# Laying the first cross-attention steps operation by operation between the last gated-slot steps of a fused decoder block, with three batches' scores in other PSUM banks

## The chip, the cores and the metric

The kernel runs on one NeuronCore of one Trainium2 chip, in one launch. The metric is the device time of that launch in microseconds. TensorE (PE; PEld is its weight load), VectorE (DVE), ScalarE (ACT), GpSimd (POOL) and SyncE (SP, which issues the DMAs) each run their own list of instructions in order, and meet only at semaphores. So the order in which a list is written, together with the waits in it, is the schedule.

## The reference

The block takes a stream `x` of 32 sequences, 128 tokens each, 128 wide, in float32:

```
x = x + slot_attention(layernorm(x))                     # 4 heads, 64 slots, a gated recurrence over time
x = x + cross_attention(layernorm(x), ctx, ctx,
        bias = fside + fside, attn_mask, key_padding)    # 16 heads of 8, softmax over 128 keys
x = x + experts(layernorm(x))                            # top 2 of 8, LoRA experts on a shared 512-wide MLP
```

The bias `fside` has its own 128x128 matrix for each batch and each of the 16 heads, so one batch brings 1 MB of it. For the cross attention of one batch that means

```
q = h @ Wq.T + bq;  k = c @ Wk.T + bk;  v = c @ Wv.T + bv          # h = layernorm(x), c = ctx
scores = q.k / sqrt(8) + attn_mask + fside + fside, -inf where padded
out = softmax(scores) @ v;   x = x + out @ Wo.T + bo
```

## The kernel before

`decoder` (L49) has three stages, one after the other: the gated-slot stage (functions `gsa_*`) works on pairs of batches, 16 in all (0 to 15); the cross stage (`x_*`) on single batches, 0 to 31; the expert stage (`f_*`) on groups of four. Each is a software pipeline. In tick `t` of the slot stage the parts belong to different pairs: `gate` works on pair t, `turn` on t-1, `intra` on t-2, `mix` on t-3, `finish` on t-4. In step `n` of the cross stage `norm` works on batch n+3, `project` on n+2, `scores` on n+1, `attend` on n and `finish` on n-1.

The functions for one engine (`gsa_tensor`, `gsa_scalar`, `gsa_vector`, `gsa_pool`, and the same for `x_`) write out one tick or step of that engine. The middle of each stage is a loop (`gsa_loop`, `x_loop`), its ends are written out by `gsa_peeled` and `x_peeled`, which switch off the parts that have no batch. The last slot ticks are 16 (turn, intra, mix, finish), 17 (intra, mix, finish), 18 (mix, finish) and 19 (finish), and the first cross steps are -3 (norm), -2 (norm, project), -1 (and scores) and 0 (and attend). I call this part the passage. In the kernel before it goes, on every engine, by whole steps: tick 16, step -3, tick 17, step -2, tick 18, step -1, tick 19, step 0, step 1, then the loop from step 2.

What the prediction follows, by engine and line:

- DVE: `statistics` and `aggregates` (L1034, L1039) and `normalise` (L1044) give a batch its normed rows, `masks` (L1051) its key mask, `score(i)` (L1026, four instructions of one head each) adds the bias to four heads' scores from one bank, `causal_attention` (L680), `slot_logits`, `slot_maxima` (L687 to L696), `causal_mix` (L714), `slot_sums` and their reciprocal (L702, L708) are the slot stage's.
- POOL: `biases` (L1121) adds mask and bias for a whole batch and writes `c_bias`; `keys_apart` (L1126) lays a batch's keys apart by head; `roots` (L1111, L1114) gives the reciprocal deviation; `slot_products` and `slot_weights` (L794, L802), `squares` (L782), `outputs_normalised` (L788) are the slot stage's. The weights of pair 15 are made in tick 17.
- PE: `all_scores` (L873) writes a batch's scores, one matmul for each of four banks; `inputs_turned` (L880), `queries_keys` (L886), `weights_turned` (L907), `mix_values` (L920), `values` (L892), `outputs` (L896) follow in a step. `attention` (L444), `slot_logits` (L453), `slot_mix` (L476), `outputs` (L486), `project_out` (L499) are the slot stage's.
- ACT: exps of the scores (L954), copies of the turned inputs (L960), keys (L971), queries (L965).
- SP: `x_loads` issues the 1 MB of bias of batch n once the bias tile of batch n-2 has been read (`need(sp, C["fm"], n - 1)`, L1150).

PSUM has eight banks here. The cross stage puts its scores in banks 1, 4, 5 and 6 and its sums in 7, and turns weights through 2 and 3. The slot stage uses 4 and 5 for attention and logits, 6 and 7 for its mix and outputs, 2 and 3 for squares, turned rows and values. Bank 6 is what the last slot pairs and the first scores both want:

```
SCORE_BANKS = (1, 4, 5, 6)                                                       # L860
pe.wait_ge(G["lgts"], PAIRS); pe.wait_ge(G["un"], PAIRS); x_peeled(cross, -1)    # L1694 to L1696
```

## Time and profile before

| | us |
|---|---|
| time, median of 3 runs | 604.25 (603.99 to 606.11) |
| profiled execution, its own time | 605.81 |
| its span, first to last instruction | 604.1 |
| a slot tick in the loop (182.46 to 171.54 on DVE) | 10.9 |
| a cross step in the loop (262.47 to 255.28 on PE) | 7.2 |
| the passage, from PE's first matmul of tick 17 to that of step 2 | 193.57 to 240.58 |

The engines are busy for 542.7 us (PE), 482.7 (DVE), 398.6 (ACT) and 355.7 (POOL) of the span. The profile lists instructions by engine, with the line, the output and input tiles, the start in us from the span's start, the duration, and in brackets how long the engine had stood idle before it and what ended that. The granted clock of TensorE is a share of full speed: 1.00 is 2.4 GHz and 0.50 is 1.2 GHz. Since every list runs in order, an instruction's start is the later of two times: when its engine is free, and when the last thing it waits for is there.

### The profile page before, as it was taken

How to read it: one execution, taken by the hardware profiler on the slowest of the kernel's cores; microseconds unless marked ns; L12 is line 12 of the kernel's file. 1: busy time of each engine (PE TensorE's matmuls, PEld its weight loads, DVE VectorE, ACT ScalarE, POOL GpSimd, SP SyncE). 2: the span in 40 equal slices, each digit the busy share in tenths (PEclk: the TensorE clock that was granted, in tenths of full speed). 3: DMA queues.
4: the chain of work that ended last, by engine and by line, in shares of the span. 5: the costliest groups of instructions: out<-in, count | busy, mean ns of one | idle time of the engine just before them, and what ended most of it. 6: DMA issues, size and time to landing. Idle time of an engine off the chain costs nothing.

```text
span 604.1 us, 17291 instructions
## 1 busy us (share of the span) xinstructions
PE 542.7 (90%) x5328; PEld 416.1 (69%) x5328; DVE 482.7 (80%) x1945; ACT 398.6 (66%) x1033; POOL 355.7 (59%) x362
## 2 busy tenths in 40 slices
PE   4689999999998559999999999999978999999986
PEld 3457777777776436777777777777766778788864
DVE  2478887887886358999999999999988688888872
ACT  2668878878775238889999999999965333333221
POOL 6234555456544657888888888888933233334430
PEclk9799999999998868999999999999987899999999
DMA  6910000000000075898989888888700000000000
GB/s 169 239 21 2 1 1 1 0 0 0 2 0 2 7 126 101 153 168 152 159 155 156 155 155 149 148 151 162 128 3 1 2 17 19 17 17 19 17 19 17
DMA packets 84429, 42.47 MB, mean 70 GB/s; under 512 B 4378, under 2 KB 84132, under 8 KB 84388
## 3 DMA queue, kind: packets, MB, share of 16 engines
q1 hardware_dynamic: 83234, 41.63, 37.5%
q8 instruction: 21, 0.34, 0.3%
q10 hardware_dynamic: 1154, 0.33, 0.2%
q14 instruction: 20, 0.16, 0.1%
HBM read 39.86 MB, written 2.10 MB: 69 GB/s over the span
## 4 chain that ended last, share of the span: by engine, by line
PE 50%; DVE 17%; issue 16%; ACT 7%; POOL 7%; DVEq 0%; ACTq 0%; POOLq 0%
PE banks L873 6%; PE banks L907 6%; PE banks L920 5%; PE banks L453 5%; ACT c_P L954 4%; PE banks L1228 4%; DVE c_P L1026 3%; DVE shared L714 3%; PE banks L1252 3%; PE banks L896 3%; PE banks L417 2%; PE banks L444 2%; PE banks L499 2%; PE banks L886 2%; DVE banks L687 2%
## 5 line engine op out<-in xcount | busy, mean ns | idle before, releaser
L1121 POOL TENSOR_TENSOR c_bias<-c_fside,c_cm 128x2048 f32<-128x2048 f32 x32 | 146.2, 4568 | 27.5 <-PE banks L873 16.9
L954 ACT ACTIVATE c_P<-c_P,c_min 128x128 f32<-128x128 f32 x512 | 156.7, 391 | 2.9 <-DVE c_min L1026 2.9
L1026 DVE CUSTOM_DVE_ANT_0 c_P<-banks,c_bias 128x128 f32<-128x128 f32 x512 | 116.4, 284 | 5.6 <-issue 3.0
L907 PEld LDWEIGHTS banks<-ident,c_P 128*128 128x128 f32 x512 | 59.3, 144 | 30.0 <-issue 23.2
L907 PE MATMUL banks<-ident,c_P 128*128 128x128 f32 x512 | 76.0, 282 | 3.7 <-DVE shared L1062 3.7
L1062 DVE COPY shared<-banks 128x512 f32<-128x512 f32 x96 | 65.7, 685 | 0.0
L1228 PE MATMUL banks<-um,lb_s 128*128 128x512 f32 x192 | 56.1, 407 | 2.7 <-ACT shared L1285 1.9
L1464 POOL TENSOR_TENSOR xs<-shared,xs 128x512 fp32r<-128x512 f32 x8 | 10.7, 1337 | 69.9 <-ACT xs L1295 69.9
L1285 ACT ACTIVATE shared<-banks,bi_col 128x512 f32<-128x512 f32 x32 | 22.0, 687 | 39.2 <-PE banks L1228 39.2
L1228 PEld LDWEIGHTS banks<-um,lb_s 128*128 128x128 f32 x192 | 34.6, 190 | 19.1 <-ACT shared L1285 12.5
L794 POOL TENSOR_TENSOR shared<-shared 128x512 f32<-128x512 f32 x16 | 20.4, 1275 | 38.1 <-ACT shared L585 38.1
L1026 DVE DVE_READ_ACCUMULATOR2_ANT c_min<- 128x1 f32 x512 | 42.6, 83 | 0.0
L873 PE MATMUL banks<-shared,c_q 32*128 32x512 f32 x256 | 38.3, 668 | 1.2 <-DVE X L727 0.5
L453 PEld LDWEIGHTS banks<-shared 128*128 128x128 f32 x256 | 29.8, 191 | 12.8 <-DVE shared L680 12.8
L920 PE MATMUL banks<-shared,c_vpad 128*32 128x128 f32 x1024 | 34.9, 277 | 0.0
L1126 POOL TENSOR_TENSOR shared<-c_k,k_mask 128x512 f32<-128x512 f32 x32 | 33.3, 1042 | 1.8 <-ACT c_k L971 1.8
L920 PE MATMUL banks<-shared,c_ones 128*32 128x128 f32 x1024 | 33.8, 273 | 0.0
L453 PE MATMUL banks<-shared 128*128 128x64 f32 x256 | 31.9, 278 | 1.7 <-DVE shared L680 1.7
L1290 ACT COPY shared<-banks 128x512 f32<-128x512 f32 x8 | 4.7, 587 | 43.6 <-PE banks L1202 43.6
L1252 PE MATMUL banks<-woT,shared 128*128 128x128 f32 x256 | 30.7, 278 | 2.1 <-DVE shared L1414 1.9
L1414 DVE SCALAR_TENSOR_TENSOR shared<-banks,neg_bi,shared 128x512 f32<-128x512 f32 x32 | 23.5, 749 | 11.0 <-PE banks L1228 10.7
L1252 PEld LDWEIGHTS banks<-woT,shared 128*128 128x128 f32 x256 | 29.2, 192 | 4.1 <-DVE shared L1414 4.1
(195 smaller groups left out, 1310.6 us busy)
## 6 DMA issues: line engine op xcount, KB each, us to landing
c_fside<-in_fside_Bx16xSxS_dram SPq DMA_DIRECT2D x64, 512.0 KB, 7.2
c_ctx<-in_ctx_dram SPq DMA_DIRECT2D x32, 64.0 KB, 5.2
out_dram<-shared SPq DMA_DIRECT2D x8, 256.0 KB, 2.3
X<-in_x_dram SPq DMA_DIRECT2D x3, 512.0 KB, 5.4
kmask_sb<-in_mask_BxS_bf_dram SPq DMA_DIRECT2D x1, 512.0 KB, 6.8
X<-in_x_dram SPq DMA_DIRECT2D x2, 128.0 KB, 3.0
c_P<-in_L_ffn_wi_dram SPq DMA_DIRECT2D x1, 256.0 KB
c_P<-in_L_ffn_lora_B_dram SPq DMA_DIRECT2D x1, 256.0 KB
```

The source lines that it names most:

```text
L453: last = nc.tensor.matmul(bank(4)[:, 256 * b + GM * h:256 * b + GM * h + GM], Am[:, 4 * (h // 2) + 2 * b + h % 2, :], sp_[:, q, b, GM * h: ...
L873: nc.tensor.matmul(bank(SCORE_BANKS[i]), qx[rows, o, :], kbd[rows, o, :, :].rearrange("p j s -> p (j s)"), start=True, stop=True).then_inc ...
L907: last = nc.tensor.transpose(bank(2 + i % 2)[:, 128 * j:128 * j + 128], P[:, q, XG * i + j, :], ident[:])
L920: last = nc.tensor.matmul(bank(7)[32 * i:32 * i + 32, 128 * w:128 * w + 128], block, PTs[:, o, i, 128 * j:128 * j + 128], start=(j == 0), ...
L954: last = nc.scalar.activation(P[:, par, h, :], P[:, par, h, :], ACT.Exp, bias=mn[:, par, h:h + 1], scale=-1.0)
L1026: last = nc.vector.tensor_tensor_reduce(out=P[:, o, h, :], in0=bank(SCORE_BANKS[i])[:, 128 * j:128 * j + 128], in1=fm[:, o, h, :], scale=- ...
L1062: nc.vector.tensor_copy(PTs[:, q, i, :], bank(2 + i % 2)).then_inc(C["ptD"], 1)
L1121: nc.gpsimd.tensor_tensor(fm[:, q, :, :], fs[:, q, :, :], bc(cm[:], XH), ALU.add).then_inc(C["fm"], 1)
L1126: nc.gpsimd.tensor_tensor(kbd[:, q, :, :], bc(kx[:], XG), inner(k_mask[:], 128), ALU.mult).then_inc(C["kbd"], 1)
L1228: last = nc.tensor.matmul(out, weight[:, a, :], moving[:, b, :], start=start and k == 0, stop=stop and k == len(PASSES) - 1, **also)
L1252: last = nc.tensor.matmul(bank(7)[:, 128 * b:128 * b + 128], hT[:, c, 128 * b:128 * b + 128], woT[:, c, :], start=(c == 0), stop=(c == FC ...
L1414: nc.vector.scalar_tensor_tensor(hT[:, c, :], bank(2 + c % 2), neg_bi[:, c:c + 1], r1[:, c, :], ALU.max, ALU.add).then_inc(M["h"], 1)
```

## The change

Each engine function takes a new argument `only`, a tuple of names, and lets a part run only if its name is in it, so that one tick or step can be laid down in several pieces. With that the passage is written out anew on all four engines:

- On POOL the bias and the keys of batch 0 come ahead of tick 17, and the bias and keys of batch 1 ahead of pair 15's slot weights, which come after them. Step -3's roots go ahead of tick 16.
- On DVE statistics, norm and mask of batches 0 and 1 stand between parts of ticks 16 and 17, and the scores of batch 0 follow straight on the slot sums of pair 15. Tick 18 is spread through steps 0 and 1, tick 19 follows step 2.
- On PE the inputs and queries of batch 0 stand before the logits of pair 15, the scores of batch 0 between slot mix and slot outputs of pair 14, and ticks 18 and 19 are spread through steps 0 to 2 with the waits that the shared banks need.
- ACT follows PE.
- The scores of batches 0, 1 and 2 go to banks 1, 4, 5, 1, so bank 6 stays with the slot stage. The fourth matmul therefore waits until DVE has read the first one's result.
- `masks` moves from the start of a step (for batch n+2) to the end of the step before (batch n+3), where the norm of the same batch is.
- Two more cross steps are written out ahead of the loop and two fewer behind it: the loop has as many rounds.

```diff
+def named(only):
+    return lambda flag, name: flag and (only is None or name in only)
...
+        FIRST_BANKS = (1, 4, 5, 1)
+        FIRST = 3
+        def score_banks(batch):
+            return FIRST_BANKS if isinstance(batch, int) and batch < FIRST else SCORE_BANKS
...
+                places = score_banks(n + 1)
                 for i in range(NI):
                     rows = slice(32 * i, 32 * i + 32)
-                    nc.tensor.matmul(bank(SCORE_BANKS[i]), qx[rows, o, :], kbd[rows, o, :, :].rearrange("p j s -> p (j s)"),
+                    if places[i] in places[:i]:
+                        need(pe, C["tt"], 4 * n + 5 + places.index(places[i]))
+                    nc.tensor.matmul(bank(places[i]), qx[rows, o, :], kbd[rows, o, :, :].rearrange("p j s -> p (j s)"),
                                      start=True, stop=True).then_inc(C["sc"], 1)
...
             def masks():
-                need(dve, C["fm"], n + 2)
-                km = kmask_sb[:, bass.ds((n + 2) * T, T)]
+                need(dve, C["fm"], n + 3)
+                km = kmask_sb[:, bass.ds((n + 3) * T, T)]
...
-            with engine.Fori(1, B // 2 - 3, 2) as m:
+            with engine.Fori(2, B // 2 - 3, 2) as m:
... POOL
             pool.wait_ge(G["xn"], PAIRS)
             x_peeled(cross, -3)
-            gsa_peeled(gsa, PAIRS + 1)
+            gsa_peeled(gsa, PAIRS)
...
             x_peeled(cross, -2)
+            gsa_peeled(gsa, PAIRS + 1, "outputs")
+            x_peeled(cross, -1)
+            gsa_peeled(gsa, PAIRS + 1, "squares")
+            gsa_peeled(gsa, PAIRS + 1, "weights")
+            x_peeled(cross, 0)
             gsa_peeled(gsa, PAIRS + 2)
-            x_peeled(cross, -1)
+            x_peeled(cross, 1)
             gsa_peeled(gsa, PAIRS + 3)
... ACT
-            x_peeled(cross, -3)
-            gsa_peeled(gsa, PAIRS + 1)
+            gsa_peeled(gsa, PAIRS + 1, "turned", "roots")
             x_peeled(cross, -2)
-            gsa_peeled(gsa, PAIRS + 2)
+            gsa_peeled(gsa, PAIRS + 1, "exps", "outputs")
             x_peeled(cross, -1)
+            x_peeled(cross, 0, "exps1", "exps2", "inputs", "exps3")
+            gsa_peeled(gsa, PAIRS + 2, "turned")
+            x_peeled(cross, 0, "exps0", "keys", "queries", "turned3")
+            gsa_peeled(gsa, PAIRS + 2, "roots")
+            x_peeled(cross, 1, "exps1")
+            gsa_peeled(gsa, PAIRS + 2, "outputs")
+            x_peeled(cross, 1, "exps2", "inputs", "exps3", "exps0", "sums", "keys", "queries", "turned3")
             gsa_peeled(gsa, PAIRS + 3)
... DVE
-            x_peeled(cross, -3)
-            gsa_peeled(gsa, PAIRS + 1)
+            x_peeled(cross, -3, "statistics", "aggregates")
+            gsa_peeled(gsa, PAIRS)
             dve.wait_ge(s_km, 16)
-            x_peeled(cross, -2)
-            gsa_peeled(gsa, PAIRS + 2)
-            x_peeled(cross, -1)
+            x_peeled(cross, -3, "normalise", "masks")
+            gsa_peeled(gsa, PAIRS + 1, "attention")
+            x_peeled(cross, -2, "statistics", "aggregates")
+            gsa_peeled(gsa, PAIRS + 1, "logits")
+            x_peeled(cross, -2, "normalise", "masks")
+            gsa_peeled(gsa, PAIRS + 1, "mix", "sums")
+            x_peeled(cross, -1, "scores0", "scores1", "scores2", "scores3")
+            gsa_peeled(gsa, PAIRS + 1, "stream")
+            x_peeled(cross, -1, "statistics", "aggregates", "values", "normalise", "masks")
+            x_peeled(cross, 0)
+            gsa_peeled(gsa, PAIRS + 2, "mix")
+            x_peeled(cross, 1, "statistics", "scores0")
+            gsa_peeled(gsa, PAIRS + 2, "stream")
...
... PE
-            x_peeled(cross, -3)
-            gsa_peeled(gsa, PAIRS + 1)
+            gsa_peeled(gsa, PAIRS + 1, "attention", "turned", "squares")
             pe.wait_ge(G["silu"], PAIRS)
             x_peeled(cross, -2)
-            gsa_peeled(gsa, PAIRS + 2)
-            pe.wait_ge(G["lgts"], PAIRS)
+            gsa_peeled(gsa, PAIRS + 1, "logits", "mix")
+            pe.wait_ge(G["shift"], PAIRS)
+            x_peeled(cross, -1, "scores")
+            gsa_peeled(gsa, PAIRS + 1, "outputs", "project")
+            x_peeled(cross, -1, "inputs", "queries", "values")
+            x_peeled(cross, 0, "scores")
+            pe.wait_ge(G["rt"], PAIRS - 2)
+            x_peeled(cross, 0, "turned0", "inputs")
+            pe.wait_ge(G["x1"], PAIRS - 2)
+            x_peeled(cross, 0, "turned1", "queries")
+            gsa_peeled(gsa, PAIRS + 2, "turned")
+            x_peeled(cross, 0, "turned2", "turned3", "values")
+            pe.wait_ge(C["ptD"], 3)
+            gsa_peeled(gsa, PAIRS + 2, "squares", "mix")
+            x_peeled(cross, 1, "scores")
+            pe.wait_ge(C["ptA"], 1)
+            gsa_peeled(gsa, PAIRS + 2, "outputs", "project")
...
+            pe.wait_ge(C["ptD"], 6)
+            gsa_peeled(gsa, PAIRS + 3, "squares")
             pe.wait_ge(G["un"], PAIRS)
+            x_peeled(cross, 2, "scores")
...
```

In the changed file the lines stand lower: L1121 is L1141, L1126 is L1146, L873 is L894, L794 and L802 are L805 and L813, L486 and L499 are L491 and L504.

The list of POOL in the passage before, from the weights of pair 15 (L794, L802) to the bias of batch 1; `shared<-shared` are tiles of the slot stage:

```order
L794 TENSOR_TENSOR shared<-shared 128x512 [waits g_ppTp,g_p]
L802 TENSOR_TENSOR shared<-shared 128x512 [waits g_ri,g_pe]
L782 TENSOR_TENSOR shared<-shared 128x256 [waits g_ss,g_un]
L1121 TENSOR_TENSOR c_bias<-c_fside,c_cm 128x2048 [waits c_cm,vector_constants_made,c_fside_loaded0,transposed_weights_copied,cross_weights_loaded]
L1126 TENSOR_TENSOR shared<-c_k,k_mask 128x512 [waits c_k]
L1111 TENSOR_TENSOR vareps<-meanvar,eps_tile 128x1 [waits c_rstd,c_aggr]
L1114 TENSOR_TENSOR rstd<-vareps,minus_half 128x1 [waits c_xn,c_vareps]
L788 TENSOR_TENSOR shared<-shared 128x256 [waits g_y,g_r]
L782 TENSOR_TENSOR shared<-shared 128x256 [waits g_ss,g_un]
L1121 TENSOR_TENSOR c_bias<-c_fside,c_cm 128x2048 [waits c_fside_loaded1,c_cm]
```

And in the changed kernel, from the bias of batch 0 to the weights of pair 15, behind which the bias of batch 2 follows:

```order
L1141 TENSOR_TENSOR c_bias<-c_fside,c_cm 128x2048 [waits c_cm,vector_constants_made,c_fside_loaded0,transposed_weights_copied,cross_weights_loaded]
L1146 TENSOR_TENSOR shared<-c_k,k_mask 128x512 [waits c_k]
L1131 TENSOR_TENSOR vareps<-meanvar,eps_tile 128x1 [waits c_rstd,c_aggr]
L1134 TENSOR_TENSOR rstd<-vareps,minus_half 128x1 [waits c_xn,c_vareps]
L799 TENSOR_TENSOR shared<-shared 128x256 [waits g_y,g_r]
L1141 TENSOR_TENSOR c_bias<-c_fside,c_cm 128x2048 [waits c_fside_loaded1,c_cm]
L1146 TENSOR_TENSOR shared<-c_k,k_mask 128x512 [waits c_k]
L1131 TENSOR_TENSOR vareps<-meanvar,eps_tile 128x1 [waits c_rstd,c_aggr]
L1134 TENSOR_TENSOR rstd<-vareps,minus_half 128x1 [waits c_xn,c_vareps]
L793 TENSOR_TENSOR shared<-shared 128x256 [waits g_ss,g_un]
L805 TENSOR_TENSOR shared<-shared 128x512 [waits g_ppTp,g_p]
L813 TENSOR_TENSOR shared<-shared 128x512 [waits g_ri,g_pe]
```

The bias of batch 0 (the first `c_bias` row) now stands ahead of all of tick 17, and pair 15's products and weights (L805, L813) have gone behind the bias and keys of batch 1.

The list of PE before, from the slot mix of pair 14 (L476) to the first scores (L873):

```order
L476 MATMUL banks<-shared 128x128 [waits g_un,g_sT,g_ppT]
L476 MATMUL banks<-shared 128x128 x7
L486 MATMUL banks<-shared 32x128 [waits g_v,g_bm]
L486 MATMUL banks<-shared 32x128 x7
L499 MATMUL banks<-g_wo_sb,shared 128x128 [waits g_v,g_onT]
L499 MATMUL banks<-g_wo_sb,shared 128x128
L873 MATMUL banks<-shared,c_q 128x512 [waits c_q,c_kbd,g_un,g_lgts]
L873 MATMUL banks<-shared,c_q 128x512 x3
```

And in the changed kernel, from the logits of pair 15 to the scores of batch 1:

```order
L458 MATMUL banks<-shared 128x64 [waits g_am]
L458 MATMUL banks<-shared 128x64 x7
L481 MATMUL banks<-shared 128x128 [waits g_un,g_sT,g_ppT]
L481 MATMUL banks<-shared 128x128 x7
L894 MATMUL banks<-shared,c_q 128x512 [waits c_kbd,c_q,g_shift]
L894 MATMUL banks<-shared,c_q 128x512 x2
L894 MATMUL banks<-shared,c_q 128x512 [waits c_tt]
L491 MATMUL banks<-shared 32x128 [waits g_v,g_bm]
L491 MATMUL banks<-shared 32x128 x7
L504 MATMUL banks<-g_wo_sb,shared 128x128 [waits g_v,g_onT]
L504 MATMUL banks<-g_wo_sb,shared 128x128
L901 MATMUL banks<-ident,c_xn 128x128 [waits c_ctx_loaded1,c_xn]
```

The first scores (L894) have moved up from behind tick 18 to behind the slot mix of pair 14. They are now three matmuls and a fourth behind a wait of its own on `c_tt`, which DVE raises when it has read the first bank.

## Rows read from the trace of the kernel before

**Rows 1.** The page: granted clock in 40 slices of the span, and the bias loads

```profile
PEclk9799999999998868999999999999987899999999
...
c_fside<-in_fside_Bx16xSxS_dram SPq DMA_DIRECT2D x64, 512.0 KB, 7.2
```

**Rows 2.** Busy time by stretch: length, busy time of each engine, clock, DMA share

```profile
193.57:240.58 47.01, 32.41 (x269) 23.16 (x269) 26.98 (x136) 21.64 (x67) 31.58 (x27) 0.78 0.41 74
240.58:283.50 42.92, 40.89 (x596) 30.93 (x596) 40.12 (x252) 38.92 (x131) 36.96 (x23) 1.00 0.91 158
213.32:217.40 4.08, 4.08 (x29) 2.06 (x29) 0.83 (x3) 0.37 (x1) 1.72 (x2) 0.52 1.03 153
225.63:231.60 5.97, 5.97 (x30) 4.43 (x30) 4.20 (x27) 2.37 (x9) 4.52 (x1) 0.56 0.51 85
```

**Rows 3.** PE's timeline: start, duration, engine, line, operation, idle time before

```profile
193.57 1.14 PE L444 MATMUL banks<-shared 64*128 64x256 f32 x8
...
197.16 2.00 PE L453 MATMUL banks<-shared 128*128 128x64 f32 x16 [1.44 <-DVE shared L680]
...
202.53 0.64 PE L486 MATMUL banks<-shared 128*32 128x128 f32 x16 [2.28 <-DVE shared L714]
...
203.75 0.42 PE L880 MATMUL banks<-ident,c_xn 128*128 128x128 f32 x1
...
213.32 1.08 PE L486 MATMUL banks<-shared 128*32 128x128 f32 x16 [4.57 <-DVE shared L714]
...
215.49 1.97 PE L873 MATMUL banks<-shared,c_q 32*128 32x512 f32 x8
217.38 0.33 PE L880 MATMUL banks<-ident,c_xn 128*128 128x128 f32 x1
...
225.63 2.09 PE L873 MATMUL banks<-shared,c_q 32*128 32x512 f32 x8 [0.52 <-DVE X L727]
...
233.42 1.14 PE L873 MATMUL banks<-shared,c_q 32*128 32x512 f32 x8 [0.36 <-issue]
...
240.58 1.14 PE L873 MATMUL banks<-shared,c_q 32*128 32x512 f32 x8
```

**Rows 4.** DVE's timeline, norm of batch 0 to first scores

```profile
194.01 0.28 DVE L1034 BATCH_NORM_STATS2 stats<-X 128x6 f32<-128x128 f32 x1
194.45 0.18 DVE L1039 BATCH_NORM_AGGREGATE meanvar<-stats 128x2 f32<-128x6 f32 x1 [0.15 <-DVE stats L1034]
...
203.11 0.20 DVE L708 RECIPROCAL shared<-shared 128x8 f32<-128x8 f32 x1
...
211.40 0.74 DVE L1044 TENSOR_SCALAR c_xn<-X,meanvar,rstd 128x128 f32<-128x128 f32 x1 [6.23 <-POOL rstd L1114]
212.06 1.21 DVE L714 TENSOR_TENSOR shared<-banks,mask_b 128x1024 f32<-128x1024 f32 x1
...
217.64 0.29 DVE L1026 CUSTOM_DVE_ANT_0 c_P<-banks,c_bias 128x128 f32<-128x128 f32 x1 [1.22 <-issue]
...
217.86 0.28 DVE L1026 CUSTOM_DVE_ANT_0 c_P<-banks,c_bias 128x128 f32<-128x128 f32 x1
```

**Rows 5.** ACT's timeline, keys of batch 1

```profile
219.79 0.35 ACT L971 ACTIVATE c_k<-banks,bk_col 128x128 f32<-128x128 f32 x1
```

**Rows 6.** POOL's timeline, slot weights of pair 15 to the bias of batch 2

```profile
202.09 1.27 POOL L794 TENSOR_TENSOR shared<-shared 128x512 f32<-128x512 f32 x1 [4.42 <-ACT shared L585]
...
205.08 4.51 POOL L1121 TENSOR_TENSOR c_bias<-c_fside,c_cm 128x2048 f32<-128x2048 f32 x1
209.56 1.03 POOL L1126 TENSOR_TENSOR shared<-c_k,k_mask 128x512 f32<-128x512 f32 x1
210.55 0.18 POOL L1111 TENSOR_TENSOR vareps<-meanvar,eps_tile 128x1 f32<-128x1 f32 x1
...
211.33 0.72 POOL L788 TENSOR_TENSOR shared<-shared 128x256 f32<-128x256 f32 x1
...
225.98 4.52 POOL L1121 TENSOR_TENSOR c_bias<-c_fside,c_cm 128x2048 f32<-128x2048 f32 x1 [2.14 <-DVE c_cm L1051]
```

More of the change, by code:

```diff
@@ L534, in gsa_normalise, with gsa_scalar @@
             last.then_inc(G["xn"], 1)
-        def gsa_scalar(act, t, par, gate, turn, intra, mix, finish, ahead):
+        def gsa_scalar(act, t, par, gate, turn, intra, mix, finish, ahead, only=None):
             def x_turned():
@@ L805, in roots_ahead, with gsa_peeled @@
                 gsa_rstd(pool, t + 1)
-            if ahead:
+            on = named(only)
+            if on(ahead, "roots"):
                 roots_ahead()
-            if finish:
+            if on(finish, "outputs"):
                 outputs_normalised()
-            if intra:
+            if on(intra, "weights"):
                 slot_products()
-            if turn:
+            if on(turn, "heads"):
                 heads_apart()
-            if intra:
+            if on(intra, "weights"):
                 slot_weights()
-            if mix:
+            if on(mix, "squares"):
                 squares()
-        def gsa_peeled(tick, t):
-            tick(t, t % 2, *(0 <= t - k < PAIRS for k in (0, 1, 2, 3, 4, -1)))
+        def gsa_peeled(tick, t, *only):
+            tick(t, t % 2, *(0 <= t - k < PAIRS for k in (0, 1, 2, 3, 4, -1)), only or None)
         def gsa_loop(engine, tick):
@@ L1698, in _ @@
+            gsa_peeled(gsa, PAIRS + 3, "squares")
+            pe.wait_ge(G["un"], PAIRS)
+            x_peeled(cross, 2, "scores")
+            pe.wait_ge(G["rt"], PAIRS)
+            x_peeled(cross, 2, "turned0", "inputs", "turned1", "mix", "queries", "turned2", "turned3", "values", "outputs")
+            pe.wait_ge(C["ptA"], 3)
+            gsa_peeled(gsa, PAIRS + 3, "project")
+            x_peeled(cross, 3, "scores", "turned0", "inputs")
             pe.wait_ge(G["x1"], PAIRS)
-            for n in range(0, 2):
-                x_peeled(cross, n)
+            x_peeled(cross, 3, "turned1", "mix", "queries", "turned2", "turned3", "values", "outputs")
@@ L1701, in _ @@
             x_loop(pe, cross)
-            for n in range(B - 6, B - 2):
+            for n in range(B - 4, B - 2):
                 x_peeled(cross, n)
```

283 lines of the change are left out of this document (146 added, 137 removed).

## The prediction

> **What bounds the kernel now.** I read the strips of the page first. The granted clock is at full level in nearly all of the span and drops in the slices that hold the passage, near slices 13 to 16 of 40 [rows 1]. The busy times by stretch say why. In the 47.01 us of the passage, from PE's first matmul of slot tick 17 to its first of cross step 2, PE is busy 32.41, DVE 26.98, ACT 21.64 and POOL 31.58. In the 42.92 us after it PE is busy 40.89 and DVE 40.12 [rows 2]. So the steady cross stage is full, and no engine is full in the passage: it is a chain that hops between engines. The timelines of the engines give the chain. PE finishes the mix of pair 15, and its slot outputs start only at 213.32, after 4.57 us without work, "released by DVE" [rows 3]. DVE's instruction ahead of that was itself held: the norm of batch 1 waited 6.23 us, until 211.40, for a reciprocal deviation from POOL [rows 4]. POOL made that at 210.55, behind 4.51 us of bias and 1.03 of keys for batch 0, and it began that bias only at 205.08, behind the slot weights of pair 15 [rows 6]. PE idle then lowers its clock: in the 4.08 us after the idle time it is granted 0.52, the lower level of 1.2 GHz, though PE is wholly busy there. The 5.97 us from 225.63 are at 0.56 [rows 2]. Slot outputs take 0.64 us at 202.53 and 1.08 at 213.32, four scores 1.14 at 240.58 and 1.97 and 2.09 earlier [rows 3].
>
> **The change part by part.** Nothing is computed that was not before. The instructions are the same but for waits. So I follow the chain through the new order and compare three milestones with the old ones: first scores on DVE (217.64), start of the bias of batch 2 (225.98), and PE's first matmul of step 2 (240.58).
>
> First leg, to the scores of batch 0. Statistics of batch 0 ahead of tick 16's attention cost that tick 0.28 + 0.15 + 0.18 = 0.6 us on DVE [rows 4]; I take 0.5 of it as late, so tick 17 starts at 194.1 instead of 193.57 [rows 3]. PE now has attention, weights, squares and then inputs and queries of batch 0 ahead of the logits of pair 15. I estimate 3.2 us of work for these (attention is 1.14 of it [rows 3]) and 0.9 of wait for ACT, which copies the inputs behind two slot parts. The logits start at about 198.2 instead of 197.16. From their start to the end of the slot sums' reciprocal the old order took 203.31 - 197.16 = 6.15 [rows 3, 4]. The new one puts norm and mask of batch 1 between, some 0.6. The reciprocal is done at 198.2 + 6.15 + 0.6 = 205.0. The scores of batch 0 follow at once, since their bias, started near 195.1 when DVE has made norm and mask, took 4.51 and was done at 199.7, and the keys at 200.7 [rows 6]. First scores: 205.0 instead of 217.64, 12.6 us earlier. Bounds: 0.5 us less late if the wait for ACT is nothing, 1 us more if the two waits add up.
>
> Second leg, to the bias of batch 2. PE has sent three matmuls and stands at the fourth, which wants bank 1 again, until DVE has read it: four heads that start 0.22 us apart (217.86 - 217.64 [rows 4]), to 205.85. Behind that matmul on PE stand the slot outputs and projection of pair 14, and then the inputs of batch 1, so this wait is on the chain. It costs 0.85 us plus the matmul of 0.3 to 0.5. Outputs and projection took 203.75 - 202.53 = 1.22 mostly at the upper clock and 215.49 - 213.32 = 2.17 at the lower one. From the inputs' turn to batch 1's keys on ACT went 220.14 - 217.38 = 2.76 [rows 3, 5], and keys apart are 1.03 on POOL [rows 6]. Together 205.85 + 0.4 + (1.22 to 2.17) + 2.76 + 1.03 = 211.3 to 212.2. POOL then makes the roots (211.33 - 210.55 = 0.78), and squares, products and weights of pair 15, which before lay one behind the other from 202.09 to 205.08, 2.99. The bias of batch 2 starts at 215.1 to 216.0 instead of 225.98: 10 to 10.9 earlier [rows 6]. What hid behind POOL before is not lost: pair 15's weights are now ready some 10 us later than before, at 215, and PE wants them in step 0 only behind the queries of batch 2, about 216 to 218.
>
> Third leg, to step 2. PE starts the scores of batch 1 at 211.4 to 212.3. Step 0 took 233.42 - 225.63 = 7.79 on PE, mostly at the lower clock [rows 3]. It gets a wait for the fourth score (0.85) and the turn of pair 15's weights, which I put like the slot outputs at 0.64 or 1.08: 9.3 to 9.7. So 220.7 to 222.0. Squares and mix of pair 15 add an estimated 1.3 to 2 (twice the slot outputs at the upper level, not quite that at the lower), to 222.0 to 224.0. Then comes the longest wait of the new order: PE puts three scores of batch 2 and needs DVE to do causal mix (1.21), statistics (0.28) and four heads (0.85) [rows 4] before the fourth. That ends at 224.4 to 226.4. The fourth, outputs and projection of pair 15 are 1.5 to 2.7 (225.9 to 229.1). The rest of step 1 is a whole step less its scores. A steady step is 7.15, from 42.92 us for six [rows 2, 3], so 6.0, and 2 more if its first half is at the lower clock. With squares of 0.5 the scores of batch 3 start at 232.4 to 237.6, against 240.58. I take the middle, 235.0, since of the waits on PE in the old order about half were followed by the lower clock and the new ones are shorter. Gain: 5.6 us. Bounds: 8.2 and 3.0.
>
> After it. Projection of pair 15 (0.6) and its addition on DVE (0.4) now lie in steps 2 and 3, where PE and DVE are nearly full, so I give back 0.7. The early masks are the same instruction in the same place of a steady step (end of one step, start of the next), so nothing there. The remaining stages are as before. The net is 5.6 - 0.7 = 4.9 us.
>
> The profiled execution took 605.81, and the median of the runs is 604.25. The sum is made within the first, 605.81 - 4.9 = 600.9, and I apply the same difference to the median: **599.4 us**.
>
> Loads are no limit. The bias of batch 2 is now issued at about 199.8 instead of 209.75, takes 7.2 [rows 1], and is wanted at 215. That of batch 4 is issued near 220 and wanted near 234. POOL's bias does not slow beside a busy DVE: 4.51 us with DVE idle at 205.08, 4.52 at 225.98 with DVE busy 4.20 of 5.97 us [rows 2, 6].
>
> **The rivals.**
>
> A. The clock stays at the upper level throughout. For it: the new waits on PE are at most 2.5 us, where the old ones before the low stretches were up to 4.57 [rows 3]. Against it: there are about six of them. The sum then ends at its lower bound, 8.2 less 0.7 to 0.0, 596 to 597.
>
> B. The clock stays at the lower level through the passage, and the kernel is slower. PE's list now alternates short pieces with waits for DVE and ACT, instead of resting once and then working densely. From 229.1, where the upper bound has PE after pair 15's projection, the remaining 6.0 us of step 1 take 12.0, and squares 1: 242.1, 1.5 later than before. With half of step 2 also at the lower clock 3.5 more and 0.7 of projection are added: 5.7 slower, 610. I put this case at 608. It decides from the point where low clock lasts past 229 into two dense steps. In the old trace 5.97 us of dense work from 225.63 at 0.56 were followed by full clock [rows 2], which speaks against it.
> By the Trainium skill (TensorE: Matmul & The Clock Gate, "A second HAM failure mode: psum-queue depth-cycling"), a PE that idles briefly and often between groups of matmuls is throttled and released again and again, and pays in throughput. By that rule the sum would lie between my upper bound and this rival, at 602 to 608; its chance is within the one I give B. The trace has so far only the other kind, one long rest and then low clock.
>
> C. What is won is taken back by the tail of pair 15. Its outputs' copy on ACT stands ahead of two groups of exps of step 1, its squares on POOL ahead of the bias of batch 3, and its roots ahead of step 2. If each holds its engine by 1.5 us more than I have, step 2 starts at 239, and the time is 603 to 604: no change. Half of the old passage's loss was of this kind (4.57 and 6.23 us [rows 3, 4]).
>
> D. The order is not what it says, because a wait on a shared bank (`g_shift`, `g_x1`) keeps the first scores where they were. Against it: `g_shift` of pair 15 is raised at about 202.4, before PE needs it. It would be 604.
>
> **How the numbers follow.** Forecast 0.56, A 0.17, B 0.09, C 0.14, D 0.04. About 0.5% (3 us) is what a measurement can tell from no change. Faster than 601.2 are A and the forecast: 0.73. Within 0.5% are D and nearly all of C: 0.17. Slower are B and the bad end of C: 0.10. The forecast's own range is 596.7 to 601.9. To hold 8 in 10 it goes a little further to both sides, from 596.0 (A) to 603.0 (part of C), and leaves out B.
>
> **What would show it.** In the profile after, DVE's first score starts near 205, POOL's bias of batch 0 near 195 and of batch 2 near 215 to 216, and PE's scores of batch 3 near 235. The length of the passage falls from 47.0 to about 41, PE's busy time in it stays about 30, and steps from 4 on are 7.15 apart as before. PE shows waits of about 2.5 us in front of the fourth score of batches 0 and 2, ended by DVE. The forecast is wrong if the bias of batch 2 starts after 219, if the clock reads 0.5 over more than half of the passage, or if steps in the loop are not 7.15.

## The result and the profile after: 676.1 us, 11.6% slower

| | before | after |
|---|---|---|
| time, median of 4 runs each, us | 605.18 (603.99 to 608.08) | 676.10 (673.88 to 676.22) |
| ratio, 95% interval | | 1.1155 [1.1107, 1.1204] |
| span of the profiled execution, us | 604.1 | 674.2 |
| mean granted clock over it | | 0.911 |

The forecast was 599.4 us, and no case of it held such a time. The passage did become shorter, by a little. About 72 us were lost behind it, in the loop of the cross stage, whose work the change leaves as it was.

The page of the kernel after, busy share and granted clock in 40 slices of the span, the queues of instruction packets (packets, MB, share of the DMA engines' time), and three groups of section 5 (busy time, mean ns, idle time ahead of them and what ended it):

```profile
DVE  2678888888765689749378385593898778888872
...
PEclk9799999999995799969869689597899789999999
...
q14 instruction: 45, 0.37, 0.2%
q8 instruction: 21, 0.34, 0.2%
...
L928 PE MATMUL banks<-ident,c_P 128*128 128x128 f32 x512 | 86.6, 307 | 59.1 <-DVE shared L1083 58.8
...
L1047 DVE DVE_READ_ACCUMULATOR2_ANT c_min<- 128x1 f32 x512 | 42.5, 83 | 25.6 <-issue 25.6
...
L1055 DVE BATCH_NORM_STATS2 stats<-X 128x6 f32 (+1 forms) x32 | 9.3, 292 | 36.2 <-issue 36.1
```

Before, the clock was at full level for the whole cross loop (the nines in slices 17 to 29 [rows 1]). Now DVE's strip falls again and again behind slice 16, and the clock falls with it. PE waits 58.8 us for DVE's copies, and DVE itself waits 36.1 and 25.6 us in two groups for nothing that the profile shows ("issue"). There are 45 instruction packets on queue 14, where the kernel before had 20; queue 8 has 21 in both.

DVE's waits in the cross loop, by the instruction that had to wait (us in total, times, longest):

```profile
DVE stats L1055 <- issue: 36.1, 5, 7.4
DVE c_min L1047 <- issue: 25.6, 5, 6.1
```

Five each, and the loop has six rounds of four steps, so five jumps back. (In the kernel before, DVE waited 1.1 us in all at its five jumps.) One of the five places of now, on DVE's timeline (start, duration, engine, line, operation, idle time before):

```profile
283.10 0.28 DVE L1072 SCALAR_TENSOR_TENSOR c_cm<-kmask_sb,half_mask 128x128 f32<-128x128 f32 x1
290.55 0.30 DVE L1055 BATCH_NORM_STATS2 stats<-X 128x6 f32 x1 [7.17 <-issue]
291.00 0.29 DVE L1047 CUSTOM_DVE_ANT_0 c_P<-banks,c_bias 128x128 f32<-128x128 f32 x1 [0.16 <-issue]
...
295.42 0.08 DVE L1047 DVE_READ_ACCUMULATOR2_ANT c_min<- 128x1 f32 x1 [3.92 <-issue]
```

The mask is the last instruction of a round and the statistics are the first of the next. Between them DVE does nothing for 7.17 us, then it runs four instructions (statistics, two heads and one read), and then nothing for 3.92. The second wait is in the middle of a pair, between a head and the read of its accumulator, where the program has no wait. Of the packets on queue 14, one falls in 287 to 288 us and one in 293 to 294, so one lies within each of the two waits. PE's timeline at the same place, and the two waits and a longer stretch by busy time (length; PE, PEld, DVE, ACT, POOL; granted clock, DMA share, GB/s):

```profile
286.54 0.71 PE L907 MATMUL banks<-c_xcT,x_wT 128*128 128x128 f32 x4
296.66 1.11 PE L928 MATMUL banks<-ident,c_P 128*128 128x128 f32 x4 [9.40 <-DVE shared L1083]
```

```profile
283.38:290.55 7.17, 3.88 (x82) 3.28 (x78) 0.00 (x0) 2.01 (x7) 4.54 (x1) 1.00 0.93 158
291.50:295.42 3.92, 0.00 (x0) 0.00 (x0) 0.01 (x1) 0.00 (x0) 0.00 (x0) 0.50 1.16 176
...
253.24:510.00 256.76, 193.83 (x2589) 145.34 (x2589) 174.99 (x1077) 170.26 (x566) 161.05 (x102) 0.85 0.63 109
```

And the stretch of the kernel before that matches the longer one:

```profile
255.28:440.00 184.72, 177.92 (x2588) 134.75 (x2588) 173.38 (x1077) 169.81 (x566) 160.88 (x102) 1.00 0.87 151
```

In the second wait no engine computes. Only the DMA engines are full. Over the loop PE is granted 0.85, where it had 1.00.

From the scores of batch 5 to those of batch 31 PE took 442.17 - 255.28 = 186.89 us before and 512.10 - 253.24 = 258.86 now, 71.97 more. DVE's two waits are 61.7 of it. The other 10.3 are not measured apart. The lower clock can account for them: the 2589 matmuls in this stretch (2588 recorded before) had 177.92 us of busy time before and have 193.83 now. Up to batch 5 the new order and an earlier start had won 2.04, and 71.97 - 2.04 = 69.93 is nearly all of the 70.1 by which the spans differ.

**The passage after.** POOL, DVE and PE:

```profile
194.21 4.52 POOL L1141 TENSOR_TENSOR c_bias<-c_fside,c_cm 128x2048 f32<-128x2048 f32 x1 [0.54 <-DVE c_cm L1072]
...
210.33 1.04 POOL L1146 TENSOR_TENSOR shared<-c_k,k_mask 128x512 f32<-128x512 f32 x1 [4.24 <-ACT c_k L992]
...
215.03 4.52 POOL L1141 TENSOR_TENSOR c_bias<-c_fside,c_cm 128x2048 f32<-128x2048 f32 x1
```

```profile
203.46 0.29 DVE L1047 CUSTOM_DVE_ANT_0 c_P<-banks,c_bias 128x128 f32<-128x128 f32 x1
```

```profile
192.56 1.13 PE L449 MATMUL banks<-shared 64*128 64x256 f32 x8
...
204.45 1.12 PE L894 MATMUL banks<-shared,c_q 32*128 32x512 f32 x2 [2.45 <-DVE c_min L1047]
...
211.47 2.08 PE L894 MATMUL banks<-shared,c_q 32*128 32x512 f32 x6
215.19 2.07 PE L894 MATMUL banks<-shared,c_q 32*128 32x512 f32 x2 [1.63 <-DVE c_min L1047]
...
224.03 0.60 PE L498 MATMUL banks<-shared,same_head 128*128 128x256 f32 x2
...
228.08 1.12 PE L894 MATMUL banks<-shared,c_q 32*128 32x512 f32 x2 [1.29 <-DVE c_min L1047]
...
237.94 1.14 PE L894 MATMUL banks<-shared,c_q 32*128 32x512 f32 x8
```

```profile
205.00:210.00 5.00, 4.39 (x28) 2.77 (x26) 2.74 (x23) 2.03 (x7) 1.09 (x1) 0.55 0.26 45
210.00:215.00 5.00, 2.85 (x8) 1.04 (x8) 3.10 (x11) 2.84 (x10) 4.51 (x6) 0.50 1.02 186
215.00:220.00 5.00, 4.82 (x15) 3.31 (x16) 1.79 (x12) 1.23 (x5) 4.55 (x2) 0.50 0.18 28
...
192.75:237.94 45.19, 35.06 (x265) 24.52 (x264) 28.04 (x134) 19.95 (x61) 30.78 (x24) 0.77 0.43 78
```

First scores and the bias of batch 2 come 14.2 and 10.95 us earlier than before [rows 4, 6], but the scores of batch 3 only 2.6 earlier (237.94 against 240.58 [rows 3]). The slot stage of this execution was itself 0.8 earlier at DVE's mask product of pair 13 (171.89 against 172.68), ahead of anything that the change moves. So the gain of the passage is 1.85 us in this execution, and its length, from PE's first matmul of tick 17 to that of step 2, is 45.4 us where about 41 was forecast. PE is at 0.50 to 0.55 for the 15 us from 205 to 220, it is at 0.72 once more in 230 to 235, and it meets a wait for the fourth score in each of the three batches.

### The profile page after: what moved, and what is told of

The parts are those of the page before. It is cut to its first block, busy times and chain, and to the rows that moved or that the text cites. A ratio compares the mean times of both kernels' runs of the same rounds, so it can differ in the third digit from the quotient of the medians.

```text
span 674.2 us, 17292 instructions
## 1 busy us (share of the span) xinstructions
PE 561.0 (83%) x5328; PEld 427.9 (63%) x5328; DVE 485.8 (72%) x1945; ACT 398.7 (59%) x1033; POOL 356.8 (53%) x362
## 4 chain that ended last, share of the span: by engine, by line
PE 54%; DVE 16%; issue 16%; ACT 10%; POOL 1%; DVEq 1%; ACTq 0%; POOLq 0%
PE banks L1250 10%; PE banks L928 6%; ACT c_P L975 5%; PE banks L941 5%; PE banks L1274 5%; PE banks L458 4%; PE banks L894 4%; DVE c_P L1047 3%; DVE shared L723 2%; PE banks L917 2%; PE banks L422 2%; PE banks L449 2%; PE banks L907 2%; DVE banks L696 1%; DVE shared L702 1%
## 5 line engine op out<-in xcount | busy, mean ns | idle before, releaser
L1141 POOL TENSOR_TENSOR c_bias<-c_fside,c_cm 128x2048 f32<-128x2048 f32 x32 | 146.0, 4563 | 33.7 <-PE banks L894 17.7
L928 PE MATMUL banks<-ident,c_P 128*128 128x128 f32 x512 | 86.6, 307 | 59.1 <-DVE shared L1083 58.8
L928 PEld LDWEIGHTS banks<-ident,c_P 128*128 128x128 f32 x512 | 65.9, 157 | 91.5 <-DVE shared L1083 58.1
L1146 POOL TENSOR_TENSOR shared<-c_k,k_mask 128x512 f32<-128x512 f32 x32 | 33.4, 1045 | 69.3 <-ACT c_k L992 69.1
L1047 DVE DVE_READ_ACCUMULATOR2_ANT c_min<- 128x1 f32 x512 | 42.5, 83 | 25.6 <-issue 25.6
L894 PE MATMUL banks<-shared,c_q 32*128 32x512 f32 x256 | 46.5, 733 | 6.6 <-DVE c_min L1047 5.4
L805 POOL TENSOR_TENSOR shared<-shared 128x512 f32<-128x512 f32 x16 | 20.4, 1277 | 34.2 <-ACT shared L591 34.2
L1055 DVE BATCH_NORM_STATS2 stats<-X 128x6 f32 (+1 forms) x32 | 9.3, 292 | 36.2 <-issue 36.1
```

The source lines that it names most:

```text
L894: nc.tensor.matmul(bank(places[i]), qx[rows, o, :], kbd[rows, o, :, :].rearrange("p j s -> p (j s)"), start=True, stop=True).then_inc(C["s ...
L928: last = nc.tensor.transpose(bank(2 + i % 2)[:, 128 * j:128 * j + 128], P[:, q, XG * i + j, :], ident[:])
L1047: last = nc.vector.tensor_tensor_reduce(out=P[:, o, h, :], in0=bank(score_banks(n + 1)[i])[:, 128 * j:128 * j + 128], in1=fm[:, o, h, :], ...
L1141: nc.gpsimd.tensor_tensor(fm[:, q, :, :], fs[:, q, :, :], bc(cm[:], XH), ALU.add).then_inc(C["fm"], 1)
L1146: nc.gpsimd.tensor_tensor(kbd[:, q, :, :], bc(kx[:], XG), inner(k_mask[:], 128), ALU.mult).then_inc(C["kbd"], 1)
```

## The experiments

Two theories were tried for the loop. F (fetch): on a jump back DVE's instructions must be loaded again, because its loop has another place in its list of instructions. An increment of a semaphore put at the head of the list is one instruction that does no work, so it only moves what stands behind it. L (layout): the new order itself, or the mask at the end of a step, makes DVE wait. In the compiled program the cross loop of DVE has 283 instructions of 64 bytes in both kernels. It begins at instruction 470 before and at 587 after. Each ratio below is to executions of the kernel before that were taken together with that run.

**e1: the order of before, only DVE's loop one round later (it begins at 586)**

```diff
-            for n in range(0, 2):
+            for n in range(0, 4):
                 x_peeled(cross, n)
-            x_loop(dve, cross)
-            for n in range(B - 6, B - 2):
+            x_loop(dve, cross, 2)          # first round; 1 before
+            for n in range(B - 4, B - 2):
```

> The kernel before, with one edit on VectorE's list alone: cross steps 2 and 3 written out ahead of the loop and two fewer behind it, so that the loop's body (283 compiled instructions) begins at instruction 586 instead of 470. Passage, banks and all other engines are as before. Theory F (fetch: after the change the body lies so over the blocks in which VectorE's instructions are loaded that each jump back finds its target gone) expects the loss of the changed kernel here too: five stalls of about 12 us on VectorE at the jump back, about 25 more loads on the instruction queue q14, and 660 to 680 us. Rival L (the new order of the passage or the banks disturb the steady cross stage) expects 604 us, no stalls, 20 loads.

Measured: 659.48 us (659.19 to 659.78), ratio 1.0888 [1.0863, 1.0913], with 45 packets on queue 14 and five waits at the jumps:

```profile
DVE c_cm L1051 <- issue: 35.7, 5, 7.3
```

Without a single instruction of the new passage, the loss is there. Here the waiting instruction is the mask, which in this order is the first of a step. So the wait goes with the jump, and not with the instruction that stands behind it.

**e2: the changed kernel with 43 semaphore increments at the head of DVE's list**

```diff
+            for _ in range(43):
+                dve.sem_inc(s_passed, 1)
             dve.wait_ge(s_x[0], 16)
```

> The changed kernel with 43 semaphore increments put ahead of VectorE's first wait, which only move its list by 43 instructions: the loop begins at 630 instead of 587, so at the same place within a block of 128 as in the kernel before (470 = 86 modulo 128, 630 = 118 modulo 128; 502 + 128 would be the same as before plus a block, so the place is 32 later than in before). F expects the stalls gone if this place is good: 600 to 604 us. If the blocks are of 256 and only the place modulo 256 counts, it may be still bad: 660 to 680. L expects 676 us in any case.

Measured: 606.68 us (604.71 to 609.29), ratio 1.0022 [1.0006, 1.0038], 20 packets on queue 14, granted clock 1.00 from 250 to 440. In 280 to 320 us this kernel has one such packet, and the changed kernel has five; in 320 to 400 this one has none:

```profile
q14 instruction: 1, 0.01, 0.1%
...
q14 instruction: 5, 0.04, 0.5%
```

Nothing of the new order was altered, and 69 us came back. F is shown and L has fallen. It also shows what the change is worth without the fetches: nothing, or a loss of 0.2%. (The expectation calls the place "the same within a block of 128"; by its own numbers, 86 and 118, it is not. The forecasts of F and L do not hang on that.)

**e8: the kernel before with 117 increments at the same place, so that its loop begins at 587**

```diff
+            for _ in range(117):
+                dve.sem_inc(s_passed, 1)
```

> The kernel before with 117 semaphore increments at the head of VectorE's list and nothing else, so that its cross loop begins at instruction 587 of the list, where the changed kernel has it. Fetch theory: the loop is fetched again at each of 6 jumps back, and the time is 655 to 680 us, with two waits per round of about 7 and 5 us on VectorE ended by nothing that the profile shows, and about 45 instruction packets instead of 20. Rival (the new order of the work itself makes the waits, or the jump of a longer prologue does): 604 to 608 us, since the order is that of before.

Measured: 664.62 us (662.93 to 666.31), ratio 1.0993 [1.0954, 1.1032], 46 packets. (Six rounds have five jumps back, not the six of the expectation.) The kernel before is slowed by place alone. Its waits, and the two of the first jump by stretch:

```profile
DVE c_cm L1051 <- issue: 34.8, 5, 7.7
...
DVE c_min L1026 <- issue: 6.6, 5, 1.6
```

```profile
279.31:284.64 5.33, 3.99 (x82) 3.28 (x78) 0.00 (x1) 2.24 (x8) 0.00 (x0) 1.00 1.11 192
285.61:287.20 1.59, 0.00 (x0) 0.00 (x0) 0.00 (x1) 0.00 (x0) 1.59 (x1) 1.00 0.00 0
```

The first wait costs about as much as in the changed kernel (7.0 us on average against 7.2), the second 1.3 instead of 5.1. In the stretch shown the DMA engines are idle in the second wait, where in the changed kernel they were full of bias loads (DMA share 0.00 against 1.16). That a fetch is slow because it comes behind the loads fits this pair, but the first wait here had the DMA engines full too (1.11) and is the shortest of the five (5.33), and no run altered the loads alone. So the cause of the longer second wait is open.

**e3 and e4: the changed kernel and the one before with DVE's loop of 2 steps per round, 12 rounds**

```diff
-            x_loop(dve, cross)
+            x_loop(dve, cross, 1)      # two steps a round on DVE alone
```

> The changed kernel, with VectorE's loop of two cross steps a round instead of four (12 rounds; body 143 compiled instructions instead of 283); the other engines' loops as they are. F expects no stall, since so short a body stays loaded wherever it lies: 600 to 604 us, the instruction loads back to about 20. What the passage alone brings then shows: the trace of the changed kernel has step 4 only 1.25 us ahead of the kernel before, when both are set on tick 14, so 603. L expects 676 us.

> The control to that: the kernel before with the same short loop on VectorE. F and L both expect 604 to 606 us: twice the jumps, at about 0.3 us each and mostly hidden.

Measured: e3 607.65 us (605.94 to 609.71), ratio 1.003 [1.0015, 1.0045]; e4 608.03 (606.86 to 610.07), ratio 1.004 [1.0026, 1.0054]. A loop of 143 instructions is not fetched again at place 587 (20 packets) and costs 0.4% in e4, where it only adds six jumps. It cures the changed kernel as the increments do, and the two differ by 0.4 us, with intervals that overlap: the new passage alone is worth next to nothing.

**e5: 11 increments instead of 43, the loop begins at 598**

```diff
+            for _ in range(11):
+                dve.sem_inc(s_passed, 1)
```

> The changed kernel with 11 semaphore increments (43 in the earlier one) at the head of VectorE's list. Its cross loop then begins at instruction 598 of the list instead of 587. Fetch theory with blocks of 8 KB (128 instructions), as the packets have it: the loop lies at place 86 of a block like in the kernel before, spans as few blocks as there, and nothing is fetched at a jump back: 605 to 608 us, no waits of 7.2 and 5.1 us. Fetch theory with blocks of 16 KB (256 instructions): place 86 of 256 against 214 in the kernel before, so the loop's 283 instructions span two blocks here as well and the result is also 605 to 608; but if one block of a pair is kept ahead, it stays at 670 to 676. Rival: not the place of the loop but something that 43 extra instructions did by their time at the start: 11 of them do a quarter of it, so 640 to 676.

Measured: 605.52 us (605.50 and 605.54), ratio 1.0016 [0.9985, 1.0046], 20 packets. Eleven places do all that 43 did, so it is a border and not the time that the increments take. For the loop of 283, places 586 (e1) and 587 are bad; 470, 598 and 630 are good. The run did not separate blocks of 8 KB from blocks of 16 KB, since both fit all five places.

That settled the 70 us. The other question was why the passage gained 1.85 us and not 5.6. Theory W: the waits for the fourth score are on the chain. Theory C: the low clock ate it. To compare kernels, I measure from DVE's mask product of pair 13.

**e6: own banks for the first scores, on top of e2**

```diff
-        FIRST_BANKS = (1, 4, 5, 1)
+        FIRST_BANKS = ((1, 4, 5, 2), (1, 4, 5, 6), (1, 4, 5, 1))
...
+            pe.wait_ge(G["rt"], PAIRS - 2)          # before the scores of batch 0
+            pe.wait_ge(G["un"], PAIRS - 1)          # before those of batch 1
+            pe.wait_ge(C["tt"], 8)                  # before the squares of pair 15
```

> The changed kernel with 43 increments at the head of VectorE's list (so without its loss in the loop, 606.7 us) and other banks for the first scores: 1, 4, 5, 2 for batch 0, 1, 4, 5, 6 for batch 1, 1, 4, 5, 1 for batch 2, with the waits on earlier readers of banks 2 and 6 that this needs. The waits of 2.45 and 1.63 us ahead of the fourth scores of batches 0 and 1 go. Theory W (these waits are on the chain that sets the end of the passage): keys of batch 1 and with them the bias of batch 2 on GpSimd start 2 to 2.5 us earlier than 215.0, scores of batch 3 at 235.5 to 236.5 instead of 238.5, time 603.5 to 605. Theory C (the low clock and the later waits on ScalarE and GpSimd set it): bias of batch 2 at most 1 us earlier, scores of batch 3 at 237.5 to 239, time 606 to 607.5.

**e7: dummy transposes where PE waits, on top of e2**

```diff
+        WARM = {-1: 10, 0: 7, 1: 6}
+        def warm(count):
+            for _ in range(count):
+                nc.tensor.transpose(bank(2)[:, 0:128], ident[:], ident[:])
...
+                        warm(WARM[n])           # before the wait for the fourth score
...
+            warm(5)                             # before the scores of batch 0
...
+            warm(4)                             # before its values
```

> The changed kernel with 43 increments at the head of VectorE's list (606.7 us) and dummy transposes into bank 2 on TensorE where it waits in the passage: 10, 7 and 6 ahead of the fourth scores of batches 0, 1 and 2, 5 ahead of the scores of batch 0 and 4 ahead of its values. Their results are never read. Theory C (the low clock of 205 to 225 us ate the gain): granted clock over 0.9 in 205 to 225, scores of batch 3 at 234 to 236 instead of 238.5, time 603 to 604.5. Theory W (the chain goes by waits for other engines, and the clock matters little): clock high, but scores of batch 3 at 238 to 239 and time 606 to 608. If the dummy work delays the work behind it and the clock stays at 0.5: 607 to 610.

**e10: of e6 only batch 0's own bank; e9: e6 with 11 dummy transposes into bank 7**

```diff
-        FIRST_BANKS = ((1, 4, 5, 2), (1, 4, 5, 6), (1, 4, 5, 1))
+        FIRST_BANKS = ((1, 4, 5, 2), (1, 4, 5, 1), (1, 4, 5, 1))      # e10
...
-            x_peeled(cross, -1, "inputs", "queries", "values")
+            x_peeled(cross, -1, "inputs")                             # e9, banks as in e6
+            warm(3)
+            x_peeled(cross, -1, "queries")
+            warm(6)
+            x_peeled(cross, -1, "values")
+            warm(2)
```

> The kernel with own banks for the first scores (600.5 us, ratio 0.994), but batch 1 again in banks 1, 4, 5, 1; only batch 0 has its own fourth bank. It tells which of the two waits was worth the 6 us. If it is batch 0's wait (behind it stand slot outputs of pair 14 and the inputs and keys of batch 1, for which GpSimd waits): ratio 0.994 to 0.997, the bias of batch 2 on GpSimd 4 to 4.6 us earlier against tick 16 of the slot stage than with the shared bank. If both matter alike: 0.998. If it is batch 1's: 1.001 or more.

> The kernel with own banks for the first scores (600.5 us, ratio 0.994) and 11 dummy transposes into bank 7 on TensorE, 3 after the inputs of batch 1, 6 after its queries, 2 after its values, where it waits for ScalarE; their results are never read. The clock there was granted 0.52 in 210 to 215 and 0.80 in 215 to 220. If short idle time still lowers the clock there and this is on the chain: clock near 1.0 in 210 to 220, scores of batch 2 to batch 3 unchanged but both 1 to 1.5 us earlier against tick 16, ratio to before 0.991 to 0.993. If the chain goes over GpSimd there (busy 28.2 of 35 us): no change, 0.993 to 0.996, or worse if the dummy work delays the scores of batch 1.

Measured, times in us; the two milestones are counted from the mask product of pair 13 and come from one execution of each kernel:

| kernel | time | ratio to before | bias of batch 2 | scores of batch 3 |
|---|---|---|---|---|
| before | | | 53.3 | 67.9 |
| changed kernel | 676.10 | 1.1155 [1.1107, 1.1204] | 43.1 | 66.05 |
| e2 | 606.68 | 1.0022 [1.0006, 1.0038] | 45.1 | 66.0 |
| e7 dummy work | 603.81 | 0.9981 [0.9960, 1.0002] | 43.4 | 64.3 |
| e10 bank of batch 0 | 601.15 | 0.9929 [0.9902, 0.9956] | 40.8 | 62.4 |
| e6 banks of 0 and 1 | 600.50 | 0.9944 [0.9920, 0.9969] | 40.5 | 58.6 |
| e9 e6 and dummy work | 600.29 | 0.9903 [0.9879, 0.9926] | 40.5 | 60.6 |

Two rows of e6, POOL's keys of batch 1, and PE's scores of batch 1:

```profile
209.74 1.04 POOL L1145 TENSOR_TENSOR shared<-c_k,k_mask 128x512 f32<-128x512 f32 x1
```

```profile
211.04 2.09 PE L893 MATMUL banks<-shared,c_q 32*128 32x512 f32 x8 [0.32 <-POOL shared L1145]
```

POOL's wait of 4.24 us for the keys is gone, because PE goes straight on to the slot outputs and the inputs of batch 1. The clock of e6, e7 and e9 by stretch, in this order:

```profile
205.00:210.00 5.00, 3.09 (x34) 1.64 (x30) 4.96 (x31) 2.85 (x10) 4.79 (x2) 1.00 1.07 174
210.00:215.00 5.00, 4.62 (x19) 2.88 (x20) 4.11 (x18) 2.62 (x10) 4.12 (x6) 0.52 0.78 148
215.00:220.00 5.00, 3.53 (x22) 3.19 (x21) 4.71 (x32) 3.92 (x13) 5.00 (x3) 0.80 0.52 75
```

```profile
205.00:210.00 5.00, 3.89 (x32) 2.52 (x31) 4.47 (x35) 0.37 (x1) 3.69 (x1) 0.84 0.84 126
210.00:215.00 5.00, 4.49 (x19) 2.81 (x17) 1.58 (x5) 4.32 (x15) 2.25 (x4) 0.50 0.50 109
215.00:220.00 5.00, 5.00 (x16) 2.33 (x12) 2.47 (x11) 0.17 (x1) 4.92 (x4) 0.50 0.76 114
```

```profile
210.00:215.00 5.00, 3.94 (x26) 2.31 (x26) 4.11 (x20) 3.68 (x13) 4.12 (x6) 1.00 0.77 148
215.00:220.00 5.00, 2.73 (x16) 1.85 (x16) 4.79 (x31) 2.76 (x8) 5.00 (x3) 1.00 0.51 74
220.00:225.00 5.00, 4.11 (x24) 2.28 (x22) 3.00 (x9) 2.06 (x6) 2.03 (x4) 0.66 0.79 154
```

How far can one execution's milestones be trusted? The bias of batch 2 differs by 2 us between e2 and the changed kernel, whose passages are the same, while their scores of batch 3 agree within 0.1. But e3 has this passage too, and its step 2 comes at 240.82 - 172.28 = 68.5, which is 2.5 later than in them. Its clock was low there:

```profile
230.00:235.00 5.00, 5.00 (x32) 3.55 (x30) 1.55 (x7) 2.24 (x8) 2.65 (x2) 0.51 0.01 3
```

So a difference under about 2.5 us in the last column says nothing, and where the milestones and the ratios disagree, the ratios of many runs decide.

W holds and was worth more than I had expected: 7.4 us at step 2 for two waits of 2.23 and 1.63, and 0.8% by the ratios (1.0022 against 0.9944). Batch 0's bank alone brings nearly all of the earlier bias of batch 2. At step 2 it brings 3.6 us of the 7.4, but its ratio is no worse than that of e6, so a gain in time from batch 1's own bank is not shown. Of C, e7 did not get the clock up beyond 210 us, so it tested only the 5 us before that. Its 1.7 us at step 2 are within what one execution can be off; its ratio is below that of e2, with intervals that just miss each other (1.0002 and 1.0006). In e9 the dummy work did keep the clock at 1.00 until 220, but it fell to 0.66 right after, and step 2 came 2.0 later than in e6. The intervals of e6 and e9 overlap (0.9920 to 0.9926), so which of them is faster is open. Both, and e10, beat the kernel before. How much of the 7.4 us is the waits themselves and how much the clock that they bring down is not separated either. In e6 there is one stretch of 5 us at 0.52 and one at 0.80, where e2 has three at the lower level (0.52, 0.50 and 0.50 from 205 to 220).

## Why the prediction was wrong

**The step that failed** is the sentence "The remaining stages are as before". I had followed the order of instructions on each engine through the passage and had taken the loop as a constant, steps 7.15 apart. The change text itself says that two more steps are written out ahead of the loop. I read that as a matter of which steps are where, and not as a shift of the loop by 117 instructions in DVE's list. In the runs this shift costs 52 us up to the scores of batch 31 with the old order (e8: 502.7 - 263.9 = 238.8 from batch 5 to 31, against 186.9) and 72 with the new one. All rivals were about the passage too, so none could reach 676. Of the signs that I had named against the forecast, "if steps in the loop are not 7.15" is the one that came true: the four steps of a round in the changed kernel take 18.9, 8.3, 7.3 and 7.2 us (scores at 282.35, 301.21, 309.48, 316.81 and 324.00).

What could have warned was on the page of before, with its 20 packets on queue 14, and in the times of those: none between 269 and 412 us, so from the first jump back on the loop ran without a fetch. A loop that runs without one is a property that a longer head can take away.
The Trainium skill has the rule ("Runtime: NRT & Kernel Launch", section "Instruction fetch mechanics"): most engines hold two blocks of 16 KiB, 256 instructions each, fetched ahead in sequence only, and a taken branch out of them stalls for a fetch. Worked out from that page's figures, as an estimate: 283 instructions lie in two blocks unless the loop begins in the last 26 places of one (2 x 256 - 283 = 229). The five places measured agree with this if a border lies 76 to 86 instructions behind a multiple of 256 in the compiled list. No run measured where the borders are. The packets here are 8 KB (0.37 MB in 45), half of that page's block. The page gives no price for such a stall.
In the changed kernel the price was 61.7 us of waits in five jumps, 12.3 each.

**Leg 1 was right.** First scores at 203.46, forecast 205.0; taken from the mask product of pair 13 the miss is 0.75.

**Leg 2 was right** in this execution; in e2, with the same passage, the bias of batch 2 came 1.9 later (45.1 against 43.1 in the table), which is past my bounds. The bias of batch 2 at 215.03, forecast 215.1 to 216.0, the wait for the fourth score 2.45 us, forecast about 2.5. The scores of batch 1 started at 211.47, forecast 211.4 to 212.3.

**Leg 3 had the right pieces and a wrong size.** Step 0 up to the squares of pair 15 took 224.03 - 211.47 = 12.6 us, where I had put 9.3 to 9.7. I had taken the old step 0 of 7.79 us [rows 3] and added one wait and one turn. It had a wait of 1.63 for its fourth score, and the clock was at 0.50 until 220. What came behind, from the squares to step 2, took 13.9, against 11.7 to 15.6 forecast. So step 2 came at 237.94 instead of 235.0, 0.3 outside my bounds. The gain was 1.85 instead of 5.6, and by steps 3 and 4 it is down to 1.2, so the give-back of 0.7 was about right. The term that was mis-sized in the passage is step 0, by about 3 us. Over the whole kernel the runs without fetches put it between 1.3 us lost (e2, ratio 1.0022) and 0.4 won (e3 against e4), that is nothing.

**The rivals.** The passage itself landed on C's figure ("step 2 starts at 239, and the time is 603 to 604: no change"), but not by C's mechanism. Pair 15's tail did hold GpSimd, whose squares stood 4.16 us for ScalarE's copy until 230.56, with the bias of batch 3 behind them. But in the changed kernel PE's scores of batch 3 did not wait for that, and in e2, e6, e7 and e10 only 0.22 us. The cause was nearer to B, PE alternating between pieces and waits at low clock: 0.50 to 0.55 until 220 and 0.72 in 230 to 235. In e3, with the same passage, it was 0.51 in 230 to 235, past the 229 that B names, and there step 2 came 0.6 later than in the kernel before (68.5 against 67.9). The Trainium skill's rule on queue cycling, weighed there, agrees with these traces in kind: e6 removes two waits of PE, and of the three stretches of 5 us at 0.50 to 0.52 one is left. D fell at once: the first scores came 14.2 us earlier.

**That the fourth score costs little** was taken without a check. I had put batch 0's wait on the chain and timed what stands behind it, but priced it by its own length, 0.85 and a matmul, and had not asked what the order would gain without it. e10 and e6 show that: the keys behind it come earlier, for which POOL stood 4.24 us in the changed kernel. Without those waits (and, in e9, with the dummy work) the order gains about what I had forecast with them: 3.4 us by the ratio of e6, 4.3 by that of e10 and 5.9 by that of e9, against 4.9.

## What to carry to other kernels

When a change writes out more or fewer steps ahead of a loop, look where each engine's loop then begins in its list and whether the trace of before shows instruction packets within it; if the loop is close to what an engine holds, shift it by a few instructions or shorten its body, and measure again before judging the change. A wait of "issue" at a jump back or between two halves of a pair, with more instruction packets than before, points to a fetch and not to the schedule. In an in-order list a reused PSUM bank costs what is queued behind its wait: try a bank of its own for the first batch before ordering anything else.

## What the runs showed of the hardware

- DVE's list is fetched in packets of 8 KB (0.37 MB in 45). At the bad place there are 25 more of them for five jumps back. The second wait of a jump took 1.6 us once with the DMA engines idle (e8) and 3.9 once with them full; why is open.
- Moving a loop of 283 instructions by 11 places changed the time by 10% (676.1 to 605.5 us). A loop of 143 at the same place has no such waits and took 607.7 us.
- PE's loop is three times as long in instructions (863), and its queue shows 21 packets in both kernels, 0.34 MB of them: no packet more for a loop that stands at another place.
- A key mask on DVE took 1.36 us at 212.73 beside POOL's squares and products, and 0.28 at 283.10. The mask of the same batch took 1.36 to 1.37 in e2, e6, e7, e9 and e10 too. No run tried why.
